# Moving the transpositions and affines of batch 1's normalised rows inside a unit of attention group 2

## The reference

```python
mod = swish(c) @ w_mod + b_mod            # shifts, scales and gates, six rows of 576 for each batch
xn  = ln(x) * (1 + sc_msa) + sh_msa
q, k, v = split_heads(xn @ w_qkv + b_qkv)
q, k = ln(q, g_q), ln(k, g_k)             # over the 36 of a head
o = softmax(q @ k.T * 36 ** -0.5) @ v
x = x + g_msa * (o @ w_proj + b_proj)
x = x + g_mlp * (gelu((ln(x) * (1 + sc_mlp) + sh_mlp) @ w1 + b1) @ w2 + b2)
```

## Time and profile before

| what | value |
|---|---|
| median of 3 runs | 2894.0 us (2893.54 to 2894.77) |
| the profiled execution | 2893.01 us |
| its span, first to last instruction | 2891.1 us |
| mean granted TensorE clock | 0.984 |
| busy: TensorE, VectorE, ScalarE, GpSimd | 96%, 69%, 53%, 24% |

### The profile page before, as it was taken

How to read it: one execution, slowest core, us unless ns; L and a number is a source line. 1 busy time by engine, 2 the same in 40 slices (tenths; PEclk the granted TensorE clock), 3 DMA queues, 4 the chain that set the end, 5 groups by cost and what they waited for, 6 DMA issues and landing times.

```text
span 2891.1 us, 43560 instructions
## 1 busy us (share of the span) xinstructions
PE 2787.1 (96%) x14764; PEld 1438.4 (50%) x14764; DVE 1996.3 (69%) x2677; ACT 1524.2 (53%) x2218; POOL 689.4 (24%) x502
## 2 busy tenths in 40 slices
PE   5579999999999999999999999989999999999999
PEld 1334444444444444444444444447575665757666
DVE  5668888888888888888888899954435344353421
ACT  2457777778887777777777777821211112121110
POOL 0143346642223333333333321010000000000000
PEclk9689999999999999999999999989999999999999
DMA  5142222222211122222223224140211202011000
GB/s 173 66 80 52 52 63 78 81 61 51 55 46 32 29 47 60 72 71 71 69 75 78 70 64 144 37 145 7 88 39 50 75 14 88 23 66 66 24 17 17
DMA packets 231121, 180.26 MB, mean 62 GB/s; under 512 B 148923, under 2 KB 176001, under 8 KB 230860
## 3 DMA queue, kind: packets, MB, share of 16 engines
q1 hardware_dynamic: 230694, 178.35, 22.4%
q10 hardware_dynamic: 296, 0.07, 0.0%
HBM read 98.77 MB, written 46.04 MB: 50 GB/s over the span
## 4 chain that ended last, share of the span: by engine, by line
PE 93%; DVE 2%; issue 1%; ACT 1%; POOL 1%; DVEq 0%; ACTq 0%; POOLq 0%
PE at_ps L1434 18%; PE at_ps L895 16%; PE at_ps L892 15%; PE at_ps L883 15%; PE at_ps L1458 15%; PE at_ps L911 10%; PE at_ps L949 1%; DVE at_plo L742 1%; PE at_ps L1424 1%; ACT at_aff L660 0%; PE at_ps L922 0%; ACT at_p L634 0%; POOL at_ssq L551 0%; PE at_ps L933 0%; ACT at_xy L608 0%
## 5 line engine op out<-in xcount | busy, mean ns | idle before, releaser
L742 DVE TENSOR_TENSOR at_plo<-at_p 128x1024 fp32r<-128x1024 f32 x1024 | 1267.0, 1258 | 199.2 <-ACT at_p L634 192.1
L634 ACT ACTIVATE at_p<-at_ps 128x1024 f32<-128x1024 f32 x1024 | 1047.0, 1025 | 406.9 <-PE at_ps L883 406.9
L895 PE MATMUL at_ps<-at_plo,at_vr 128*37 128x512 f32 x2048 | 1072.1, 591 | 0.0
L892 PE MATMUL at_ps<-at_p,at_v 128*73 128x512 bf16 x2048 | 796.3, 389 | 0.7 <-DVE at_plo L742 0.7
L1434 PE MATMUL at_ps<-ml_w2s,ml_hid 128*128 128x288 f16 x3456 | 428.1, 286 | 2.0 <-issue 2.0
L1458 PE MATMUL at_ps<-ml_xhi,ml_w 128*128 128x512 f16 x1296 | 399.2, 381 | 3.5 <-issue 3.5
L1434 PEld LDWEIGHTS at_ps<-ml_w2s,ml_hid 128*128 128x128 f16 x3456 | 338.0, 98 | 86.9 <-issue 2.5
L892 PEld LDWEIGHTS at_ps<-at_p,at_v 128*73 128x73 f16 x2048 | 232.7, 114 | 241.0 <-DVE at_plo L742 2.3
L537 POOL TENSOR_TENSOR at_tssq<-at_tssq,head_eps 128x8 f32<-128x8 f32 x112 | 124.0, 1107 | 924.3 <-DVE at_tssq L712 924.3
L895 PEld LDWEIGHTS at_ps<-at_plo,at_vr 128*37 128x37 f32 x2048 | 233.5, 114 | 222.5
L911 PE MATMUL at_ps<-wq,at_xhi 128*128 128x432 f16 x1008 | 297.6, 350 | 19.1 <-DVE at_txc L716 18.5
(11 more groups left out here) (150 smaller groups left out, 2313.6 us busy)
## 6 DMA issues: line engine op xcount, KB each, us to landing
head_sums<-at_oT SPq DMA_DIRECT2D x256, 72.0 KB
ml_held<-head_sums SPq DMA_DIRECT2D x64, 256.0 KB
at_xy<-in_L_cond_w SPq DMA_DIRECT2D x34, 288.0 KB
w_halves<-wq SPq DMA_DIRECT2D x68, 144.0 KB
at_xy<-in_x SPq DMA_DIRECT2D x32, 288.0 KB, 2.8
ml_x<-in_x SPq DMA_DIRECT2D x8, 1152.0 KB, 5.6
out<-ml_x SPq DMA_DIRECT2D x7, 1152.0 KB, 4.5
wm<-in_L_cond_w_mod SPq DMA_DIRECT2D x6, 1152.0 KB, 13.9
```

The source lines that it names most:

```text
L634: act.activation(p[:, s % NP, :], ps[:, 2 * (s % 2):2 * (s % 2) + 2, :].rearrange("p a n -> p (a n)"), ACT.Exp).then_inc(exp_done, 1)
L742: nc.vector.tensor_tensor(plo[:, s % NP, :], p[:, s % NP, :], high, ALU.subtract).then_inc(plo_ready, 1)
L892: nc.tensor.matmul(acc[0:VW, bass.ds((U % 2) * CH, CH)], v16[:, h % 2, 2 * s + a, 0:VW], high, start=(s == 0 and a == 0), stop=False, skip ...
L895: last = nc.tensor.matmul(acc[0:RW, bass.ds((U % 2) * CH, CH)], vr[:, h % 2, 2 * s + a, 0:RW], plo[:, s % NP, a * CH:(a + 1) * CH], start= ...
```

## The change

In group 2 the transpositions of columns 0 to 3 move from step 4 to step 3 on TensorE and that of column 4 from step 7 to step 5. ScalarE's four affines move from step 5 to step 4, its fifth affine and the high part from step 7 to step 5. VectorE's low part stays in step 7. No instruction and no semaphore is added or taken away.

```diff
@@ scalar: unit
+                    if G == HATS_IN and s == 4:
+                        hats(u, range(KF))
                     if G == HATS_IN and s == 5:
-                        hats(u, range(KF))
-                    if G == HATS_IN and s == 7:
                         hats(u, (KF,))
                         hats_high(u)
@@ tensor: attend
-                    if G == HATS_IN and s == 4:
+                    if G == HATS_IN and s == 3:
                         hat_turns(u, range(KF))
-                    if G == HATS_IN and s == 7:
+                    if G == HATS_IN and s == 5:
                         hat_turns(u, (KF,))
```

## The result

The changed kernel takes 2904.6 us (median of 6 runs, 2903.27 to 2905.74) against 2893.77 us for the kernel before beside it: 10.8 us slower, a ratio of 1.0039 (95% interval 1.0026 to 1.0051). The forecast was 2906.0, in a range of 2899 to 2912. The profiled execution took 2904.87 us, with a span of 2903.0.

What follows compares the result with a forecast made beforehand. Bound: the chain in group 2 from step 6's exponential through its low part and the normalisation to the next product. 12 x 0.83 + 4 x 0.52 = 12.0 us slower gave 2906.0 us, range 2899 to 2912.

Steps and rivals of the forecast that it cites:

- What bounds the kernel: Group 2: products wait for exp6, its low part and the normalisation; period 14.19 us, 13.97 without any wait.
- Steps (1) and (2): Four turns ahead of scores(4) start exp4 0.33 us later; four affines ahead of exp5 put it at P+10.00.
- Step (3): TensorE at the fifth turn: a new wait for the fourth affine, 0.53 us, scores(6) at P+10.65, not setting the end.
- Step (4): ScalarE behind exp5: turn's result ready 0.11 us ahead of the fifth affine; with the high part, exp6 comes 0.83 later.
- rival A: TensorE's new wait at the fifth turn becomes the bound; 16.6 us, 2910.6, if its result is 0.4 later; chance 0.10.
- step (5): Unit's end: the product follows exp6 by 2.84 us, at P+15.02, so twelve units grow by 0.83 each.
- Step (6): Unit's edge: exp7 and the next exp0 (14.06 rather than 14.42) are relieved and the high part done earlier, worth nothing.
- The head units: Four of 16 units, with GpSimd copying a head: VectorE's low parts and the casts hold each other, 0.52 us growth each.
- The load of xy: SyncE's load lands by P+5.96, ahead of the turns at P+6.65; stays hidden with 0.7 us left of 2.0.
- Rival B: Idle time pays for the work ahead of exp6, which comes at most 0.3 later; under 5 us, 2897; chance 0.12.
- C (faster): ScalarE's lateness at the unit's edge holds the products; freed, all waits go: -5.1 us, 2889; chance 0.02.

Runs made afterwards that it cites:

- `first_half`: Kernel before with only the transpositions of columns 0 to 3 moved to step 3 and their affines to step 4; 2887.93 us, ratio 0.9981.
- `turns_early`: Kernel before with only the transpositions of columns 0 to 3 moved to step 3 on TensorE, ScalarE untouched; 2892.96 us, ratio 0.9996.
- `high_late`: Changed kernel with the high part alone moved back to step 7; 2896.37 us, ratio 1.0011 to the kernel before.
- `late_padded`: Kernel before with three meaningless ScalarE copies added behind the high part in step 7; 2893.32 us, ratio 1.0000.
- `fifth_in_six`: Changed kernel with the fifth transposition, fifth affine and high part in step 6 instead of step 5; 2889.98 us, ratio 0.9986 to the kernel before.

## Why the prediction was right, point by point

- What bounds the kernel: right. A plain period follows exp6 by 2.80 to 2.84, or is TensorE's own 13.97 plus its stalls, whichever is later; `first_half` reaches 13.99, where the prediction said a unit without waits would be. A head unit follows exp6 by more (3.35 before, 3.04 in the changed kernel), the unit behind it by less (2.73 and 2.70). Two readings of the rows were off without harm. Exp6 is the first of the pair from 643.82, not the second; the sums do start from 643.82. And the units behind a head unit were 14.07 to 14.10 before, so eight units, not twelve, were like the one shown.
- Steps (1) and (2), exp4 0.33 later and exp5 at 10.00: right to 0.01. `turns_early` shows step (1) by itself: the 0.65 of idle time splits into 0.22 and 0.35.
- Step (3), a stall at the fifth turn: there, but mis-sized. The prediction called it 0.53, from TensorE's arrival to the load of the turn's weights. By its own times scores(6) at 10.65 are 0.76 behind the 9.89 that they need without a wait; they came at 10.36, 0.47 behind. The hand-over that I had taken from VectorE to TensorE (0.17) is 0.05 from ScalarE, and scores(6) followed the load of the weights by 0.17, not 0.34.
- Step (4), the turn's result just in time for the fifth affine, by 0.11: the margin was mis-sized. The turn ended at 645.19, P+10.52, 0.29 earlier than reckoned: 0.12 of it is the shorter hand-over, and 0.17 is that a turn whose weights had to wait starts its matmul with them (0.33 from there, not 0.50). The margin is about 0.4, and rival A, as I had put it, was farther off than the 0.10 it got. But its other form, the stall as TensorE's own bound, is only 0.5 us a unit behind the chain, as `high_late` shows. Between the two, 0.29 behind the chain, lies exp6's other way, through scores(0). The prediction had numbers for these in step (5) (scores(0) held until 13.37, last sums at 14.72, product at 15.02) and named neither as what comes next.
- Step (5), exp6 0.83 later and the product 2.84 behind it: 0.81 and 2.80. VectorE starting 1.05 rather than 1.08 behind exp6 is half of the difference. In the traces the twelve units without a head's copies grew by 9.06 us in all, where the sum has 9.96, and the head units by 1.90, where it has 2.08. That is 10.96 for 12.0; the medians differ by 10.8.
- Step (6), nothing is gained at the unit's edge: right; `late_padded` puts 0.8 us more there for nothing, in the kernel before.
- The head units: 0.47 to 0.49 instead of 0.52 (the first from 14.70 to 15.19). The reasoning held in detail: the first cast was kept back until P+12.31, where the low part of step 5 ends, and the low part of step 6 ended at 664.30, 1.08 behind the end of the second cast.
- The load of xy: hidden. The turns carry no wait for it, at 641.32 as at 656.28, in the whole of group 2.
- Rival B (absorbed) and C (faster) fall with the period of 14.96 and `late_padded`.

What beats both kernels is half of the change: turns in step 3 and affines in step 4, with the fifth part left in step 7, at 2887.93 us. Group 2 is then within 0.5 us of TensorE's own work, so by this trace there is nothing more to win from the order inside its units.

## What to carry to other kernels

When work moves inside a repeated step, list what stands between two points of the critical chain on each in-order engine before and after; work that moves in ahead of such a point delays it by its length, less the idle time that it fills. Here two instructions of 0.62 and 0.63 came in, 0.43 of ScalarE's idle time went (0.65 before, 0.22 after), and exp6 moved by 0.81. Behind exp6, in `fifth_in_six`, the same work cost nothing. A change of two parts should be priced, and run, as two: here one part alone gains 5.7 us, and with the other added the whole is 10.8 slower than before. A stall that something else hides still has a price of its own, which shows as soon as the cover goes.

## What the runs showed of the hardware

Between a GpSimd cast and a VectorE operation with two SBUF inputs, 0.03 us decided who waits: with both starting at 659.09 the low part took 1.75 us, with a lead of 0.03 it took 1.23 and the cast 1.72. Where the cast led by 0.29, the low part took 1.46. The Trainium skill, SBUF — State Buffer, Who interferes with whom, says that the first to start wins and the other is blocked; the traces agree, and add that here it moved the period of a head unit by 0.5 us (14.70 against 14.20) with no change of either operation. With two VectorE operations back to back, the one-element GpSimd instruction beside the first took 0.62 us instead of 0.19, and the cast behind it 1.67 instead of 0.67 beside the second. And a transposition that had waited for its operand was done 0.33 us after its weights began to load (644.86 to 645.19), where in the stream of the kernel before it took 0.50 (644.75 to 645.25).
